# GNN block on one core: setup loads and stores reordered on their queues, later key stores issued inside the first edge pass, chunk links computed on 51 partitions

## What is computed

```python
# layer 1 and 2 (GAT): for every edge
alpha = leaky_relu(a_src[src] + a_dst[dst] + a_edge)      # 8 heads
m = segment_max(alpha, dst); alpha = exp(alpha - m[dst])
out = segment_sum(xs[src] * alpha / (segment_sum(alpha, dst)[dst] + 1e-16), dst) + bias
h1 = layer_norm(elu(out) + h0)
# message layer: for every edge
em = relu(layer_norm(concat(x[src], x[dst]) @ msg_w + msg_b)) * edge_weight
messages = segment_sum(em, dst) / count
```

## Time and profile before

| | us |
|---|---|
| median of 3 runs | 7129.88 (7124.65 to 7131.47) |
| the profiled execution, its own time | 7131.2 |
| its span in the trace | 7129.4 |
| setup, until PE's first instruction of the first pass | 185 |
| first pass, until POOL's last gather of it | 185 to 2200 |

### The profile page before, as it was taken

The page is one execution under the profiler, slowest core; times in us unless marked ns, Lnnn a source line. Parts: engine busy times, 40 slices in busy tenths (PEclk is TensorE's granted clock), DMA queues, the critical chain, the costliest instruction groups (busy, mean ns, idle before and its releaser), DMA issues. The chain is left out here.

```text
span 7129.4 us, 144008 instructions
## 1 busy us (share of the span) xinstructions
PE 5259.0 (74%) x35340; PEld 4587.9 (64%) x35340; DVE 4850.1 (68%) x15294; ACT 2931.9 (41%) x9954; POOL 4844.7 (68%) x4953
## 2 busy tenths in 40 slices
PE   2788888888885288888988999354777777777762
PEld 1677667676764277777877888344666666666652
DVE  3677777777776556665666666656777777777776
ACT  1344444444442222222222222233666666666652
POOL 2677777777773377777777777215777777777764
PEclk7798999989997566666666666577999899999986
DMA  8444444444443222222222222302232333332330
GB/s 168 106 116 116 116 116 116 116 116 116 116 116 78 57 62 64 63 63 63 63 64 63 63 63 62 82 19 80 80 80 80 80 80 80 80 80 80 80 82 18
DMA packets 369255, 595.99 MB, mean 84 GB/s; under 512 B 105841, under 2 KB 254722, under 8 KB 368500
## 3 DMA queue, kind: packets, MB, share of 16 engines
q0 software_dynamic: 208064, 494.30, 27.4%
q1 hardware_dynamic: 151968, 88.86, 4.9%
q10 hardware_dynamic: 8469, 3.62, 0.2%
HBM read 547.82 MB, written 44.22 MB: 83 GB/s over the span
## 5 line engine op out<-in xcount | busy, mean ns | idle before, releaser
L954 POOL DMA_INDIRECT arena<-rows,slot_src x3232 | 3087.1, 955 | 1056.3 <-issue 960.6
L739 POOL DMA_INDIRECT arena<-msg_rows,slot_src x1624 | 1537.0, 946 | 534.5 <-issue 494.6
L1666 PE MATMUL psum<-arena 128*128 x3248 | 805.3, 333 | 509.8 <-DMA arena<-msg_rows,slot_src 498.8
L1141 ACT ACTIVATE arena<-psum 128x512 f32<-128x512 bf16 x808 | 481.8, 596 | 1572.2 <-PE psum L995 1566.1
L1035 PE MATMUL psum<-arena 128*128 128x145 f32 x3232 | 954.6, 386 | 0.0
L1282 DVE TENSOR_TENSOR arena<-arena,psum 128x290 f32 x1616 | 730.0, 452 | 317.1 <-DVE arena L1282 305.9
L1666 PEld LDWEIGHTS psum<-arena 128*128 128x128 f32 x3248 | 543.3, 210 | 578.3 <-issue 577.9
L1037 PE MATMUL psum<-arena 128*128 128x145 f32 x3232 | 875.8, 361 | 0.0
L1050 PE MATMUL psum<-arena 128*128 x3232 | 679.1, 342 | 265.5 <-DVE arena L1262 211.6
L1404 DVE TENSOR_TENSOR arena<-arena,psum 128x129 f32 x1616 | 468.4, 290 | 540.2 <-PE psum L1729 461.7
L1050 PE MATMUL psum<-a_src_a_dst,arena 128*128 x3232 | 633.9, 315 | 183.6 <-DVE arena L1262 145.6
(11 more groups left out here) (268 smaller groups left out, 9509.7 us busy)
## 6 DMA issues: line engine op xcount, KB each, us to landing
arena<-rows,slot_src POOLq DMA_INDIRECT x3232
arena<-msg_rows,slot_src POOLq DMA_INDIRECT x1624
arena<-slot_keys SPq DMA_DIRECT2D x100, 128.0 KB
edge_alpha<-arena SPq DMA_DIRECT2D x50, 128.0 KB
arena<-edge_alpha SPq DMA_DIRECT2D x50, 128.0 KB
h<-arena SPq DMA_DIRECT2D x2, 3136.0 KB, 17.7
arena<-rows SPq DMA_DIRECT2D x2, 3136.0 KB, 13.3
slot_keys<-arena SPq DMA_DIRECT2D x24, 256.0 KB
```

Source lines behind the costliest of these rows:

```text
L739: pool.indirect_dma_start(out=self.buffer[:, v % U, j, :], out_offset=None, in_=self.source, in_offset=bass.IndirectOffsetOnAxis(ap=K.SRC[ ...
L954: pool.indirect_dma_start(out=E.rowbuf[:, r, j, :], out_offset=None, in_=E.source, in_offset=bass.IndirectOffsetOnAxis(ap=K.SRC[:, at:at + ...
L1666: pe.matmul(psH[b][:, j, :], onehotT[:, b, j, :], K.by_dst[:, bass.ds(blocks(v, j), 1), :].rearrange("p b w -> p (b w)"), start=True, stop ...
```

## The change

It edits `prepare`, `chunk_links`, `edge_side_loads` and the places of some tensors:

- The DRAM copy of x into `rows1` moves from ACT's queue to SP's, behind `edge_rows`. The layer 2 weights, the `enc_w1` loads, the message weights, two vectors and the encoder bias (34 DMAs) move behind `node_rows`' stores on SP's queue. The other 12 vectors and `gate_b` move behind the store of the links. At the end of `prepare` `rest_in` isn't waited for any more; SP waits for it before the loads of group 2.
- The ends are stored per chunk, not per slot (two arrays of 818: 8 DMAs, 1616 elements), loaded back four times as 51 x 16, shifted as needed, and `chunk_links` works on 51 partitions with nine instructions.
- Of the keys only those of the first 128 slots are stored in the setup (2 DMAs). The other 26 are issued by SP in the pass, before the loads of group 2.

```diff
--- before.py
+++ after.py
@@ -55,7 +55,7 @@
 DCOL1 = F + H + 2
 AW = F + H + H + 1
 REGION = -(-max(NB * ROW1, NW * WCOL) // 64) * 64
-ARENA = 3 * REGION + 4160
+ARENA = 3 * REGION + 3480
 
 fp32, bf16, i32, i16, u8 = mybir.dt.float32, mybir.dt.bfloat16, mybir.dt.int32, mybir.dt.int16, mybir.dt.uint8
 ALU = mybir.AluOpType
@@ -197,7 +197,6 @@
         self.stage = R[:, at:at + NB * (ROW1 - F)].rearrange("p (b w) -> p b w", b=NB)
         at += NB * (ROW1 - F)
         self.h0 = table(R, F, at)
-        self.ends = R[0:1, at:at + 5 * 832].rearrange("a (k q) -> a k q", k=5)
         at += NB * F
         SW = SC * P
         lanes = lambda a: R[:, a:a + SW].rearrange("p (c e) -> p c e", e=P)
...
@@ -262,7 +264,7 @@
 
     K.by_dst = table(K.RL, DCOL1)
     K.keys = K.dram("slot_keys", [2, (NW + 1) * CH * H * P])
-    key_ends = K.dram("slot_key_ends", [2, SC, P])
+    firsts, lasts = K.dram("chunk_firsts", [NW * CH + 2]), K.dram("chunk_lasts", [NW * CH + 2])
     K.links = K.dram("chunk_links", [NW, 4 * CH + 2])
     K.wt_dram = K.dram("slot_weight", [P, SLOTS])
     edge_rows = K.dram("edge_rows", [EROWS, 3, P], i32)
@@ -290,6 +292,7 @@
     cleared.done(pool.memset(K.SRC[:, SLOTS:], 0))
     cleared.done(pool.memset(K.DL[:, SLOTS:], -1.0))
     cleared.done(pool.memset(T.block, 0))
+    cleared.done(pool.memset(T.chain, -BIG))
     cleared.done(pool.memset(pair_words[:, :], 0))
     cleared.done(pool.memset(K.Vbd[:, :, :, :], 0.0))
     for to in (K.to_right, K.to_left, K.carry):
@@ -306,34 +309,17 @@
     if E - full < P:
         load(sp, rows_in, edge_rows[TILES - 1:TILES, :, E - full:P], T.pad[0:1, :, E - full:P])
     load(sp, rows_in, edge_rows[TILES:EROWS, :, :], T.pad[1:EROWS - TILES + 1, :, :])
-    load(sp, keys_first, row_of(K.keys[0, NW * CH * H * P:NW * CH * H * P + H * P]), T.minus_five)
-
-    def attention_weights(relay, l):
-        load(act, relay, (T.W1 if l == 1 else K.W2)[:, 0:F], D[f"L0_gnn_lin_w{l}_T"])
-        load(act, relay, T.lin[:, l - 1, :], D[f"L0_gnn_lin_w{l}"])
-        load(act, relay, T.edge[:, l - 1, :], D[f"L0_gnn_lin_edge_w{l}"])
-        for k, what in enumerate(("src", "dst", "edge")):
-            load(act, relay, T.att_col[:, 3 * (l - 1) + k:3 * (l - 1) + k + 1],
-                 D[f"L0_gnn_att_{what}{l}"].rearrange("h (c a) -> (h c) a", a=1))
-
-    attention_weights(first_in, 1)
+    load(sp, sent, K.rows1[N:NPAD, 0:F], K.by_dst[LAST:P, NB - 1, 0:F])
+    load(sp, sent, K.rows1[0:N, 0:F], D["x"])
+
+    attention_weights(K, T, D, act, first_in, 1, T.W1)
     load(act, first_in, T.W1[:, F + 2 * H:], D["L0_gnn_in_w_T"])
     load(act, first_in, T.encw2, D["L0_gnn_enc_w2"])
     load(act, first_in, T.encb2, column(D["L0_gnn_enc_b2"]))
     load(act, first_in, K.vec["L0_gnn_in_b"], row_of(D["L0_gnn_in_b"]).broadcast_to([P, F]))
-    load(act, sent, K.rows1[0:N, 0:F], D["x"])
-    load(act, sent, K.rows1[N:NPAD, 0:F], K.by_dst[LAST:P, NB - 1, 0:F])
-    attention_weights(rest_in, 2)
-    for c in range(CH):
-        load(act, rest_in, T.w1_rep[4 * c:4 * c + 4, :], D["L0_gnn_enc_w1_T"])
-    for c in range(CH // 2):
-        load(sp, rest_in, K.b1rep[HID * c:HID * c + HID, :], column(D["L0_gnn_enc_b1"]))
-    for n in K.vec:
-        if n != "L0_gnn_in_b":
-            load(sp, rest_in, K.vec[n], row_of(D[n]).broadcast_to([P, F]))
-    load(sp, rest_in, K.WM[:, 0:2, :], D["L1_gnn_msg_w"].rearrange("(s f) o -> f s o", s=2))
-    load(sp, rest_in, K.WM[:, 2:4, :], D["L1_gnn_upd_w"].rearrange("(s f) o -> f s o", s=2))
-    load(sp, rest_in, K.gate_b[:, :], row_of(D["L1_gnn_gate_b"]).broadcast_to([P, 1]))
+    load(act, keys_first, row_of(K.keys[0, NW * CH * H * P:NW * CH * H * P + H * P]), T.minus_five)
+    load(act, keys_first, row_of(lasts[0:1]), T.minus_five[:, 0:1])
+    load(act, keys_first, row_of(firsts[NW * CH + 1:]), T.minus_five[:, 0:1])
 
     made.after(dve, pe)
     fold.done(dve.tensor_copy(K.ident_bf[:, :], K.ident[:, :]))
@@ -344,7 +330,7 @@
     filled.after(dve)
     blocks_of_slots(K, T, place)
     place.after(pool, sp)
-    rows_in.after(pool, act)
+    rows_in.after(pool)
     with nc.allow_non_contiguous_dma("block of each slot, once"):
         for k in range(2):
             load(sp, block_out, blk_dram.rearrange("(c m k) -> m c k", m=HALF, k=2)[:, :, k], T.blk_i[k * HALF:(k + 1) * HALF, :])
@@ -363,6 +349,16 @@
     fold.after(pe)
     keys_first.after(dve, act)
     evacuated, copied, squared, multiplied = node_rows(K, T, sent, h0_out)
+    rows_in.after(act)
+    attention_weights(K, T, D, sp, rest_in, 2, K.W2)
+    for c in range(CH):
+        load(sp, rest_in, T.w1_rep[4 * c:4 * c + 4, :], D["L0_gnn_enc_w1_T"])
+    load(sp, rest_in, K.WM[:, 0:2, :], D["L1_gnn_msg_w"].rearrange("(s f) o -> f s o", s=2))
+    load(sp, rest_in, K.WM[:, 2:4, :], D["L1_gnn_upd_w"].rearrange("(s f) o -> f s o", s=2))
+    for n in ("L1_gnn_msg_b", "L1_gnn_upd_b"):
+        load(sp, rest_in, K.vec[n], row_of(D[n]).broadcast_to([P, F]))
+    for c in range(CH // 2):
+        load(sp, rest_in, K.b1rep[HID * c:HID * c + HID, :], column(D["L0_gnn_enc_b1"]))
     evacuated.after(pe, pool)
     copied.after(pe)
     squared.after(pool)
@@ -386,38 +382,24 @@
     place.step(dve, lambda: dve.scalar_tensor_tensor(T.valid, T.local, float(P), T.valid, ALU.is_lt, ALU.mult))
     place.step(dve, lambda: dve.scalar_tensor_tensor(T.dstf, T.dstf, 1.0, T.valid, ALU.add, ALU.mult))
     place.after(sp, act)
...
+    whole, left, singles = SLOTS // P, (NW - 1) * WS % P // 2, SLOTS - (NW - 1) * WS
+    with nc.allow_non_contiguous_dma("both ends of every chunk, once"):
+        for of, k, e in ((firsts, 0, 0), (lasts, 1, P - 1)):
+            lanes = T.dstf[k * HALF:(k + 1) * HALF, :, e:e + 1]
+            load(sp, ends_out, of[1:1 + whole * HALF].rearrange("(c m a) -> m c a", m=HALF, a=1), lanes[:, 0:whole, :])
+            load(sp, ends_out, column(of[1 + whole * HALF:1 + whole * HALF + left]), lanes[0:left, whole, :])
+            for k1 in range(2):
+                load(sp, ends_out, of[1 + (NW - 1) * CH:1 + NW * CH].rearrange("(m k a) -> m k a", k=2, a=1)[:, k1, :],
+                     T.dstf[k1 * HALF + left:k1 * HALF + left + singles // 2, whole, e:e + 1])
+    keep_keys(K, T, keys_first, 0)
+    ends_out.after(sp)
+    keys_first.after(sp)
+    Q = NW * CH
+    for k, of in enumerate((firsts[1:Q + 1], firsts[2:Q + 2], lasts[1:Q + 1], lasts[0:Q])):
+        load(sp, ends_in, T.ends[:, k, :], of.rearrange("(z c) -> z c", c=CH))
     srcs.after(pe)
     slot_columns(K, turned, wts, T.WT, T.erow[:, :, 2, :], act, 8)
-    edges.keys_first, edges.keys_rest = keys_first, keys_out
-    ends_out.after(sp)
     h0_out.after(sp)
...
     wts.after(sp)
     load(sp, wt_out, K.wt_dram, T.WT)
 
@@ -431,9 +413,44 @@
     h0_out.after(dve)
     wts.after(dve)
     chunk_links(K, T, links_out)
+    for n in K.vec:
+        if n not in ("L0_gnn_in_b", "L1_gnn_msg_b", "L1_gnn_upd_b"):
+            load(sp, rest_in, K.vec[n], row_of(D[n]).broadcast_to([P, F]))
+    load(sp, rest_in, K.gate_b[:, :], row_of(D["L1_gnn_gate_b"]).broadcast_to([P, 1]))
+    edges.keys_rest, edges.rest_in, edges.setup = keys_out, rest_in, T
     for relay in (made, filled, cleared, fold, place, srcs, words, wts, turned, evacuated, copied, squared, multiplied, copied_a,
-                  rest_in, links_out, wt_out, sent, h0_out):
+                  links_out, wt_out, sent, h0_out, keys_first):
         relay.after(pe, act, dve, sp)
+
+
+def attention_weights(K, T, D, queue, relay, l, W):
+
+    load(queue, relay, W[:, 0:F], D[f"L0_gnn_lin_w{l}_T"])
+    load(queue, relay, T.lin[:, l - 1, :], D[f"L0_gnn_lin_w{l}"])
+    load(queue, relay, T.edge[:, l - 1, :], D[f"L0_gnn_lin_edge_w{l}"])
+    for k, what in enumerate(("src", "dst", "edge")):
+        load(queue, relay, T.att_col[:, 3 * (l - 1) + k:3 * (l - 1) + k + 1],
+             D[f"L0_gnn_att_{what}{l}"].rearrange("h (c a) -> (h c) a", a=1))
+
+
+def keep_keys(K, T, relay, c):
+
+
+
+    sp, whole = K.sp, SLOTS // P
+    left, singles = (NW - 1) * WS % P // 2, SLOTS - (NW - 1) * WS
+    for k in range(2):
+        if c < whole:
+            at = c * HALF * H * P
+            load(sp, relay, K.keys[k, at:at + HALF * H * P].rearrange("(m h e) -> m h e", h=H, e=P),
+                 T.dstf[k * HALF:(k + 1) * HALF, c, :].unsqueeze(1).broadcast_to([HALF, H, P]))
+        else:
+            lanes = T.dstf[k * HALF:k * HALF + left + singles // 2, c, :].unsqueeze(1).broadcast_to([left + singles // 2, H, P])
+            at = c * HALF * H * P
+            load(sp, relay, K.keys[k, at:at + left * H * P].rearrange("(m h e) -> m h e", h=H, e=P), lanes[0:left, :, :])
+            at = (NW - 1) * CH * H * P
+            load(sp, relay, K.keys[0, at:at + singles * H * P].rearrange("(m k h e) -> m k h e", k=2, h=H, e=P)[:, k, :, :],
+                 lanes[left:, :, :])
 
 
 def blocks_of_slots(K, T, place):
@@ -615,22 +632,21 @@
 
     dve, sp = K.dve, K.sp
     s = K.relay("links_steps")
```

(32 more changed lines are left out.)

38 lines of the change are left out of this document (7 added, 31 removed).

## The result

| | us |
|---|---|
| changed kernel, median of 4 runs | 7077.64 (7075.77 to 7079.27) |
| kernel before, median of 4 runs beside it | 7127.26 (7124.10 to 7131.47) |
| ratio, 95% interval | 0.993 [0.9913, 0.9947] |
| profiled execution of the changed kernel, its span | 7077.72, 7075.9 |
| PE's first instruction of the pass (S), before and after | 184.95, 134.69 |

A forecast was written before the change was run, and what follows sets the result against it. POOL's gathers bound the first pass, whose end moves one for one with its start S. Ten steps, mostly along SP's queue, bring S from 184.95 to 130: 7131.2 - 55 = 7076, range 7056 to 7102.

The forecast's parts named there:

- step 8: SP's stores of the ends and first keys until landed: 14 us in all, bounds 10 and 22.
- Steps 1 and 3: SP's edge arrays take half, 12 us; copy of x at full rate 16.6 plus 5 us, next issue at 50.
- step 4: Block numbers out and back until the first store of `rows1`: 17.5 us as before, to 67.
- Step 6: SP's queue behind the `h0` store: next small DMA held 11 us, to 93; bounds 0.5 and 11.6.
- step 9: Ends loaded back 3.5 us, `chunk_links` 2 us, links' store until PE 2.3 us: S = 130.
- Step 10: 26 key stores behind the start: 51.5 us at 1.98 each, group 2 loaded about S + 115, cost 0.
- Steps 1 to 7: Setup from the edge arrays through the 34 small loads, on SP's and ACT's queues: SP through at 108.
- Each queue with its own pace: Rival: edge arrays keep 24 us and the copy 33 on SP's queue; S = 153, time 7099, chance 0.15.
- Slow small loads: Rival: 0.85 us for each of 34 loads and 22 us for the ends; S = 152, time 7098, chance 0.15.
- Faster copy and stores: Rival: five stores take 10 us, no hold after `h0`, gathers cost the copy nothing; S = 110, 7056, chance 0.15.
- Late keys: Rival: key stores slowed beside gathers in the pass, group 2's keys 122 us late; time 7178, chance 0.03.
- No effect: Rival: something else, above all the landing of `rows1`, holds the start; within 0.2%, chance 0.04.

The follow-up runs named there:

- the two controls: The changed kernel unaltered, rerun on the second and third chips: 7092.04 us beside 7145.44 for the kernel before, and 7082.84 beside 7133.95.
- the last run: Changed kernel with block numbers and ends transposed by PE before storing, small loads and `h0` on ACT's queue behind its computing: 7052.90 us, ratio 0.9884.
- the first experiment: Changed kernel with the 26 later key stores back in the setup, ahead of the loads of the ends: 8863.30 us, ratio 0.9962 to its kernel before.
- the threefold stores: Changed kernel with each later key store in the pass followed by two more into spare tensors: 7109.64 us, 17.6 over the control.

## Why the prediction was right, step by step

The forecast was 7076, the median 7077.64. Its frame held: of POOL's waits for a buffer only the one at the start of the pass shrank, and a microsecond at S is a microsecond of the time (36.3 for 35.9, 27.8 for 28.8, 31.5 for 29.9 us). Of the 55 us 50.3 came; what is missing is mainly one term, step 8.

| step | forecast | measured |
|---|---|---|
| 1 edge arrays done, first gather of POOL | 27, 32 | 28.0, 32.37 |
| 2 `node_rows` starts, keys ready | 24, 71 | 24.02, 73 |
| 3, 4 block numbers out, `rows1` stores start | 50, 67 | 56, 69.5 |
| 5, 6 `h0`, next DMA accepted | 82, 93 | 82.5, 95 |
| 7 34 loads | 15 | 13.6 |
| 8 ends and first keys | 14 | 19.6 |
| 9 ends back, links, to PE | 3.5 + 2 + 2.3 | 2.9 + 1.4 + 2.1 |
| S | 130 | 134.7 |
| 10 26 key stores, keys of group 2 | 51.5, S + 115 | 31.2, S + 93 |

**Steps 1 and 3, the engines shared.** Halving was right: 12.7 us beside nothing, 24.7 beside the copy. In step 3 the queue took the block numbers 6 us later than forecast. Of these 4 came back in step 4: the 17.5 us taken from the earlier trace rows held 4.38 us of issuing, and from the end of the issue it is 13.5 us to the first store of `rows1`, after 13.1 before.
**Step 6, the queue held behind `h0`.** Of the two bounds, 0.5 and 11.6, the upper was taken and 11.9 measured; where the order was kept, the other runs have 12.1 to 13.2.

**Step 8 is the mis-sized term.** I scaled 3328 elements in 17.5 us to 1616 in 8.5. Half the elements did not land in half the time: from the first store to the load 19.6 us, 19.2 and 15.1 in the two controls. The bounds of 10 and 22 held it. S was 4.7 us late: 0.7 from the ends' store at 108.65 and 5.6 from this term, less 1.3 in step 9 and 0.2 that the sum had rounded up. Turned into rows the same step is 9.9 us (15.0 in the last run, with `h0` beside it), so it is largely the scattered elements that cost; what sets the pace of one of them is open.

**Step 10: the cost of 0 was right and its size was not.** The stores take 1.20 each beside gathers; the 1.98 came from the earlier trace rows, where 28 took 55.50. A third of that was no property of the key stores: in the setup of the first experiment, 28 took 36.17. What slowed them before is open. Part of it are the ends' elements, beside which the first of them ran (from 108 to 128 us q1 moved only 0.04 MB). But alone, too, they went at 181 GB/s, against 256 in the first experiment, though the engines weren't idle in either (95.8% and 99.3%). The source was then a part of `arena` and is now the tensor `lane_keys`; no run swaps that alone.

**What the total hides: the reordering.** Steps 1 to 7 work out what the new order of loads does, as if S hung on it. With the old order the time is the same to 0.9 us: the saving of ACT's 36 us (60.15 to 24.02) was spent on SP, which had to carry the copy, `h0` and 34 loads ahead of the ends. It could have been read from the sum itself: the ends' store stood at 108 in it, and at 106.21 in the earlier trace rows. The whole gain lies behind that store.

**The anchor.** The sum was set against the profiled execution's 7131.2, near the slow end of before's runs (7124.10 to 7131.47). The profiled pair differs by 53.5 us, 3.2 more than S: it is 51.2 at POOL's last gather of the first pass and 56.2 at its first of the second (2443.45 and 2387.30). The stage between the two took 244.4 us before and 239.4 after, and 239.6 to 245.5 in eight other traces, so that is scatter. From the median, the 55 us would have given 7072. So two errors hid each other: 4.7 us too much gain and a starting point 3.9 us too high. That 7076 came within 1.6 us is luck to that extent.

**The rivals.** Each queue with its own pace: refuted (12.7 and 24.7 us). Slow small loads: 13.6 us, refuted; its other half, the ends at up to 22 us, nearly came (19.6). Faster copy and stores: 12.9 us for the five stores, between the 15 of the sum and its 10, but the queue did hold and the copy was slower than in the sum, not faster. Late keys: not within 32 us, and the threefold stores show what they would have cost. No effect: S fell and the time with it; `rows1` let POOL start at 90.44, as the sum had it (about 90).

## What to carry to other kernels

Before a reordering is credited, write down the time at which the common next step happens, in the old order and in the new: here it was 106 and 108 us, and the reordering was worth nothing. Where two costs run over each other, as bulk stores and the landing of small ones did, remove each alone and then both: the keys' move was worth 39 or 21 us and the ends and links 32 or 14, depending on whether the other had been done. A queue with a 3 MB transfer in it is a wait for the next DMA, however small, so what the critical path needs goes ahead of it or on the other queue, and elements scattered over partitions are turned into rows before they are stored.
